# A graph-network kernel on one core: 288 instead of 176 of 464 gathered pairs are placed in the first 416 slots of the first pass, and VectorE's wait for the copied sums moves to its first sum

## The reference, cut to what matters

```python
h = jnp.maximum(_layernorm(x), 0.0)                 # 6250 x 128
deg = segment_sum(1, dst) + 1;  dinv = rsqrt(deg)
s = segment_sum((h * dinv)[src], dst)               # first pass: one row of 128 floats per edge
h1 = ((s + h * dinv) * dinv) @ W1 + b1              # as the kernel orders it: sum first, then W1
```

## Time and profile before

| what | us |
|---|---|
| median of three runs | 3008.43 |
| the profiled execution's own time | 3004.23 |
| its span, first to last instruction | 3002.3 |
| first pass, first weights of VectorE to the last sum | 112.35 to 919.6 |
| slots 32 to 415, flush to flush | 269.16 |
| slots 416 to 463 | 43.66 |
| slots 464 to 815 | 434.55 |

### The profile page before, as it was taken

The page is one execution under the profiler, slowest core; times in us unless marked ns, Lnnn a source line. Parts: engine busy times, 40 slices in busy tenths (PEclk is TensorE's granted clock), DMA queues, the critical chain, the costliest instruction groups (busy, mean ns, idle before and its releaser), DMA issues.

```text
span 3002.3 us, 63571 instructions
## 1 busy us (share of the span) xinstructions
PE 2551.4 (85%) x16470; PEld 2230.5 (74%) x16470; DVE 2110.1 (70%) x6760; ACT 1728.0 (58%) x3864; POOL 1756.9 (59%) x1812
## 2 busy tenths in 40 slices
PE   4577779988888888887899999999999977878776
PEld 2344448888886778777788888888888867777776
DVE  6788876556535677777765666766676667878777
ACT  7777666666666666676754444444444454444444
POOL 5476676556303777777702766666665047777773
PEclk9699999999999899999999999999999989999998
DMA  4355555555552344444413444444444154344433
GB/s 129 123 194 183 189 185 204 211 196 192 187 194 75 106 125 131 130 117 130 130 57 104 145 132 133 134 140 124 143 124 131 56 180 130 116 128 130 130 115 111
DMA packets 185629, 419.88 MB, mean 140 GB/s; under 512 B 36655, under 2 KB 136700, under 8 KB 175533
## 3 DMA queue, kind: packets, MB, share of 16 engines
q10 hardware_dynamic: 83703, 244.23, 23.1%
q0 software_dynamic: 61472, 140.49, 17.5%
q1 hardware_dynamic: 40118, 31.23, 3.3%
HBM read 311.35 MB, written 102.16 MB: 138 GB/s over the span
## 4 chain that ended last, share of the span: by engine, by line
PE 53%; POOL 14%; issue 10%; DMA 9%; DVE 6%; ACT 5%; ACTq 3%; SPq 1%; DVEq 0%; POOLq 0%
PE ps L1185 15%; POOL rows L633 14%; PE ps_high L1176 9%; PE ps L1115 8%; DMA rows<-table,edge_src 7%; PE ps_high L1185 7%; ACT tab_area L803 4%; PE ps_high L1132 3%; PE ps L1095 3%; PE ps_high L1127 2%; PE ps_high L1265 1%; ACTq L412 1%; PE ps L1298 1%; DVE tab_area L1599 1%; DMA acc<-counts 1%
## 5 line engine op out<-in xcount | busy, mean ns | idle before, releaser
L633 POOL DMA_INDIRECT rows<-table,edge_src x1664 | 1668.1, 1002 | 933.5 <-SPq L531 396.0
L1185 PE MATMUL ps<-tab_area,acc 128*128 128x129 f32 (+2 forms) x6370 | 1039.9, 311 | 5.4 <-DVE acc L1654 3.0
L1185 PEld LDWEIGHTS ps<-tab_area,acc 128*128 128x128 f32 x6370 | 915.9, 202 | 49.6 <-DVE acc L1654 5.8
L1176 PE MATMUL ps_high<-rows,weights 128*128 x2784 | 611.1, 333 | 218.1 <-SPq L528 93.4
L1176 PEld LDWEIGHTS ps_high<-rows,weights 128*128 128x128 f32 x2784 | 460.0, 199 | 294.5 <-DVE weights L1641 114.4
L904 ACT ACTIVATE step<-xbuf,rows 128x128 f32 x928 | 356.8, 394 | 534.6 <-PE ps_high L1176 387.3
L803 ACT ACTIVATE tab_area<-ps_high x816 | 403.3, 494 | 205.6 <-PE ps_high L1132 169.9
L1654 DVE TENSOR_TENSOR acc<-acc,ps_high 128x258 f32 (+1 forms) x938 | 332.0, 354 | 206.6 <-PE ps_high L1176 195.3
L1115 PE MATMUL ps<-acc 128*128 128x128 f32 x2450 | 338.9, 283 | 47.5 <-issue 27.7
L1115 PEld LDWEIGHTS ps<-acc 128*128 128x128 f32 x2450 | 313.4, 197 | 55.1 <-issue 48.7
L1585 DVE TENSOR_TENSOR xbuf<-xbuf,ps 128x128 f32 x489 | 139.1, 284 | 268.8 <-PE ps L1095 216.9
(11 more groups left out here) (249 smaller groups left out, 3051.1 us busy)
## 6 DMA issues: line engine op xcount, KB each, us to landing
acc<-counts ACTq DMA_DIRECT2D x105, 1120.0 KB
counts<-tab_area ACTq DMA_DIRECT2D x51, 1568.0 KB
acc<-counts ACTq DMA_DIRECT2D x25, 1568.0 KB
rows<-table,edge_src POOLq DMA_INDIRECT x1664
table<-tab_area SPq DMA_DIRECT2D x6, 903.0 KB, 4.8
table<-acc SPq DMA_DIRECT2D x7, 448.0 KB, 5.0
table<-tab_area SPq DMA_DIRECT2D x6, 455.0 KB, 4.3
table<-tab_area SPq DMA_DIRECT2D x6, 448.0 KB, 3.0
```

The lines of the kernel that those rows point to most:

```text
L633: nc.gpsimd.indirect_dma_start(rows[:, t % UNROLL, 0:row_floats[k]], None, tables[k], bass.IndirectOffsetOnAxis(ap=edge_src[:, t:t + 1], a ...
L1176: nc.tensor.matmul(ps[DENSE_BANKS + m % PAIR_BANKS][:, 0:WIDTH[k]], weights[:, m % W_RING, :], rows[:, bass.ds(known["slots"][m % UNROLL], ...
L1185: ins = nc.tensor.matmul(dense_sum(k, j), gate_blocks[:, n % S_RING, j * PART:(j + 1) * PART], table[:, h, 0:WIDTH[k]], start=(h == 0 and ...
```

## The change

Two edits. `PAIRS_EARLY` becomes 288, so that 288 of the 464 pairs stand in the slots up to 416 and 176 in the slots after it. And VectorE's wait for `sums_begun` moves from the front of the pass into `add_pair`, ahead of the first sum (m = 0).

```diff
-PAIRS_FROM, PAIRS_EARLY = 2 * FLUSH, 176
+PAIRS_FROM, PAIRS_EARLY = 2 * FLUSH, 288
...
             v.wait_ge(half_rows_ready, 2)
             v.wait_ge(acc_cleared, 4)
-            v.wait_ge(sums_begun, 2)
 
             def first_pass():
...
                     if m % QUAD == 0 and m // QUAD + 1 < PAIR_QUADS:
                         weigh(m // QUAD + 1)
                         load_nodes(m + 2 * QUAD)
+                    if m == 0:
+                        v.wait_ge(sums_begun, 2)
                     v.wait_ge(pairs_done[0], m + 2)
                     add(node_of(m), ps[m % FIRST_BANKS][:, 0:FEAT])
```

## The result

The changed kernel takes 3034.68 us (median of four runs, 3028.3 to 3035.39), the one before 3006.88 beside it (its median was 3003 to 3007 in all comparisons but the last): a ratio of 1.009, 95% interval 1.007 to 1.0109. So it is slower, by 28 us; 3045 was forecast. The profiled execution took 3034.89 us, its span 3032.9, 30.6 more than before.

What follows compares the result with a forecast made beforehand. POOL's gathers were to bound slots 32 to 415, PE slots from 464 on. +70 - 4 - 1 - 27 = +38 on 3004.23 us gave 3042, 3046 against the median, called 3045; range 3027 to 3066.

Steps and rivals of the forecast that it cites:

- The direction and the bound: Whole kernel slower, 3045 us; in slots 32 to 415 POOL becomes the bound, 0.916 us a slot.
- the handoffs: Slots 32 to 415: engines waiting for each other in a ring, 0.789 us a slot after the change, below POOL's need.
- The signs named ahead: First stretch: flushes 14 to 15 us apart, POOL busy about 0.77, few SyncE waits, TensorE waiting at L1095, gathers' mean 0.94 to 1.1 us.
- Slots 32 to 415: POOL's 261 gather intervals at 1.293 us plus 4 us for the last tile: slot 415 ends 70 us later.
- thirty gathers: From 412.05 to 449.55 us POOL issued 30 gathers without waiting, taken as its own pace: 1.293 us a gather.
- a possible saving of 16 us: First stretch: if fewer VectorE marks per gather ended the stretching of gathers wholly, 261 x 0.06 us would come off.
- The wait: Start of the pass: without the wait for copied sums at the front, slots begin 4.1 us earlier, bounds 0 and 4.1.
- Slots 416 to 463: Fewer pairs: first 32 slots 4 us shorter, last 16 only 1 us because a 12 us DMA stays.
- Slots 464 to 799: 98 fewer pairs on PE, the bound, at 0.28 us each: 27 us shorter, bounds 25 and 34.
- the clock recovers: Rival, slots 464 to 799: with fewer pairs no clock dips, 23 us more back, about 3022 us; chance 0.08.
- POOL stays hidden: Rival, first stretch: tiles stay landed ahead, handoffs set 12.62 us per 16 slots; total 3002 or 3006 us; chance 0.07.
- Bursts: Rival, first stretch: waits paid on top of POOL's time, at most +98, total 3072 to 3076 us; beyond that bound 0.05.

Runs made afterwards that it cites:

- the experiment meant for it: 288 early pairs, wait moved, loads moved, plus a 128-column POOL memset and wait ahead of each first-pass gather: 3340.83 us, against 3325.02 without the memset.
- E2: Only the pairs changed, 288 early instead of 176, wait in its old place, against the kernel before: 3030.06 us, ratio 1.0095.
- E1: Only the wait moved, 176 early pairs kept, against the kernel before: 3000.83 us against 3003.44, ratio 0.9996 (0.9986 to 1.0007).
- e5: 176 early pairs, wait moved, TensorE's L406 loads behind the fourth and eighth pair instead of third and sixth: 2954.12 us, ratio 0.9844 to the kernel before.
- e11: As e5 but 288 early pairs: 3325.02 us, ratio 1.0169 to the kernel before, which took 3268.03 us in that comparison.

## Why the prediction came out right, and where it was not

**The direction and the bound: right, the nearness of the sum: luck.** POOL's gathers, not the handoffs, carry the changed first stretch. This rests on readings of the trace, not on the experiment meant for it, which couldn't show it: POOL hardly waits for a free tile, TensorE has new waits for L528, the lead is five where it was nine, and the chain runs over the gathers. E2 shows that the pairs make the whole slowdown. The signs named ahead hold for the first stretch: flushes 14.8 us apart, POOL busy 0.77 of the time, a mean gather of 1.03 us. But the end of slot 815 missed by only 6 us because the first stretch was 15 us too short in my sum and the last 22 us too long.

**Slots 32 to 415, 70 forecast, 84.9 measured.** The 11th gather came at 133.65 instead of 132.75 (+0.9). From it to the 272nd, at 483.08, are 261 intervals of 1.339 us, where I had taken 1.293 from thirty gathers (+12). The flush came 6.2 us behind the last one, not 4 (+2). The pace was too short because the thirty were a fair stretch: the earlier trace rows already gave 1.31, and the mean gather grew from 1005 to 1033 ns. Here I had leaned on the Trainium skill (SBUF — State Buffer, "Who interferes with whom") for a possible saving of 16 us, since VectorE's marks per gather become fewer. The trace does not agree with that use: per gather there are fewer marks and the gathers are longer. Those that overlap a mark (L1598, one line lower than before) do last longer, 1062 ns in the mean against 990 for the others, and fewer of them do, 158 of 266 where it was 147 of 172; but both kinds grew, from 1010 and 972, and what stretches them is not known.

**The wait: -4.1 forecast, -2.0 measured, and worth nothing in the end.** I had TensorE's first counting step at about 107, as soon as the marks are there, and put its own register loads at nothing. They hold it until 113.22, so ScalarE still waited 1.50 us for its second window. And setup ran 1.1 us later (VectorE's last work on the table started at 100.77 for 99.65). E1's interval includes no change.

**Slots 416 to 463: right or nearly so** (-3.8 and -0.4, for -4 and -1). The flush and read back of slot 447 are the fixed part, as said.

**Slots 464 to 799: the mis-sized term, -48.8 for -27.** The mechanism named, fewer pairs on a full TensorE, is real but smaller than I priced it. With the loads moved 252 pairs take 373.40 us; 21 groups without a pair take 21 x 15.76 = 331. The difference over 252 is 0.17 us a pair, not 0.28, and 98 pairs are worth 17 us; e5 and e11 side by side, over two comparisons, give 12. The other 32 to 37 of the 48.8 come from the loads, which fall out of step with the flushes when 252 becomes 154. I had the sign of it in front of me as a rival, "the clock recovers", and gave it 0.08 with the words that nothing in the rows said why the dips should go. A timeline of TensorE's queue would have said it: two long loads behind each flush, and a stall of up to 2.1 us at every second one. The average over 21 groups (19.94 us) hid that every second group was long (the earlier trace rows shows one of each kind and I read the difference as the clock's).

**The rival "POOL stays hidden" was priced too kindly.** It put the handoffs at 12.62 us per 16 slots, 34 us more for 112 pairs. Carried on from 176 and 232 pairs ((302.91 - 270.34)/56 = 0.58 us a pair, 0.67 on the last part), the handoffs alone would have cost 65 to 75 us. So by this estimate, which goes on beyond 232 pairs in a straight line, most of the first stretch's 87 us is what a pair costs in that ring anyway, and POOL adds only some 12 to 22. One group of 16 slots right behind a change of density was no measure of a pace.

**Bursts.** The upper bound of the first stretch, 98, was not reached.

## What to carry to other kernels

When work of one kind is spread evenly over slots and something else comes at a fixed count of slots, look for a common period before pricing a density: small instructions (here loads of loop numbers into registers) can meet the same burst of DMA each time, and then the count of the work explains nothing. Look for two such instructions in a row: here one long load alone cost nothing, and two close together cost 1.3 to 2.1 us. Test it by moving the small instruction, not the work; in e5 two lines gave 1.6% where moving 112 pairs lost 0.9%. And to tell whether a producer has become the bound, count how far it is ahead of its consumer in the trace before and after, rather than its busy share.

## What the runs showed of the hardware

- A load of eight or two numbers into TensorE's registers (L406) takes 0.59 us in the median of 61 and up to 2.48 beside full DMA engines (before, slots 464 to 799). With one such load long at a time, 1.7 to 2.0 us, TensorE had enough work in hand (e5, 20 cases); two long ones 0.19 to 0.25 us apart made it stand still 1.3 to 2.1 us (before, 10 cases).
- ScalarE's loads stretch in the same moment: L412 took 877 ns on its queue at 687.9, against a median of 313 in that stretch. At the start, beside the stores of the table, four loads of TensorE took 1.1 to 2.2 us each (after).
- Behind TensorE's stall of 1.94 us the granted clock was 0.50 from 694 to 696 and 0.69 from 696 to 698. That is 2 x 0.50 + 2 x 0.31 = 1.6 us of full clock lost on top of the stall.
- A memset of 0.11 us on POOL between two gathers costs nothing: gathers that stood 1.25 us apart still do. One of 0.22 us with a wait makes it 1.44.
- In the last comparison the kernel before took 8.8% longer. It was not traced there, but e11 was, and what could be compared had its old length: a gather's median was 945 ns, and the 15.76 us group of the earlier trace rows was 15.76 again. Waits grew where engines hand work to each other. From the end of a pair on TensorE to the start of its sum, where VectorE had stood idle, it was at most 0.15 us in e5 (38 cases between 150 and 400 us); in e11 the median was 0.20 and a quarter were over 1.1 (82 cases). Only some 63 of the 290 us that e11 takes over the changed kernel lie ahead of the end of slot 815 (977.6 for 914.5). The cause is not known.
